# A double layernorm, a two-way Mamba and six transformer layers on one core: Mamba drives of five states by ScalarE and transposes, preceding rows by transfers, a mask in eight products, and met waits between the output products of 68 tiles

## The reference

```
u = layernorm(layernorm(x))                      # the second one affine
for direction in (forward, backward):            # 8 Mamba passes: 4 batches x 2
    xp, z = split(u @ W_in);  xc = silu(conv4(xp) + b)          # 256 channels each
    dt = softplus(...);  B, C = ...              # from xc @ W_x; 16 states
    h[n, t] = h[n, t-1] * exp(dt * A[n]) + (dt * xc) * B[n, t]  # n = 0..15
    y = sum_n h[n, t] * C[n, t] + xc * D;  out_d = (y * silu(z)) @ W_out
x = x + layernorm(x) + 0.5 * (out_f + out_b);  r = layernorm(x)
for layer in range(6):                           # 16 heads of 64
    s = r with the second 64 features taken from the token before
    q, k, v = heads of s @ Wqkv;  q, k = l2norm, scale, rotary
    sim = 8 * q k^T, over a window of 32 tokens and the one before it, masked
    r = r + softmax(sim) v @ Wo;   r = r + gated_feed_forward(layernorm(shifted r))
out = x + r
```

## Time and profile before

| | before |
|---|---|
| runs, median (lowest to highest) | 3920.66 us (3914.4 to 3925.08), 3 runs |
| span of the profiled execution | 3921.5 us |
| busy share: PE, PEld, DVE, ACT, POOL | 95%, 64%, 85%, 74%, 83% |
| first and last scan of the Mamba part | 80.7 us, 1007.9 us |
| first and last score of the transformer part | 1072.7 us, 3864.9 us |

### The profile page before, as it was taken

How to read it: one execution, slowest core, us unless ns; L and a number is a source line. 1 busy time by engine, 2 the same in 40 slices (tenths; PEclk the granted TensorE clock), 3 DMA queues, 4 the chain that set the end, 5 groups by cost and what they waited for, 6 DMA issues and landing times.

```text
span 3921.5 us, 110568 instructions
## 1 busy us (share of the span) xinstructions
PE 3707.5 (95%) x43392; PEld 2518.5 (64%) x43392; DVE 3319.6 (85%) x3407; ACT 2915.4 (74%) x6890; POOL 3241.5 (83%) x2370
## 2 busy tenths in 40 slices
PE   7889989988789999999999999999999999999997
PEld 2333333333377777777777777777767777777775
DVE  4999999999688888888888887888878888788885
ACT  7555445553388887888888887888878888888885
POOL 3888888888698888888888888888888888888883
PEclk8999998998899999999999999999999999999999
DMA  1221222212100000000000000000000000000001
GB/s 68 73 76 70 76 71 75 76 71 83 50 16 2 16 3 2 17 2 16 3 6 13 2 16 2 6 13 3 16 2 6 13 2 16 2 6 2 2 3 44
DMA packets 31567, 102.12 MB, mean 26 GB/s; under 512 B 4676, under 2 KB 6600, under 8 KB 30928
## 3 DMA queue, kind: packets, MB, share of 16 engines
q1 hardware_dynamic: 31056, 95.05, 7.0%
HBM read 90.32 MB, written 4.72 MB: 24 GB/s over the span
## 4 chain that ended last, share of the span: by engine, by line
PE 68%; issue 2%; ACT 2%; DVE 0%; POOL 0%; POOLq 0%; ACTq 0%; DVEq 0%
PE ps L1116 17%; PE ps L1043 13%; PE ps L1105 9%; PE ps L1054 8%; PE ps L1093 7%; PE ps L1141 5%; PE ps L1154 3%; PE ps L1078 2%; PE ps L1065 1%; PE ps L1123 1%; PE ps L1129 1%; ACT prob L1246 0%; PE ps L1023 0%; ACT mixed L1255 0%; ACT w_qk L1175 0%
## 5 line engine op out<-in xcount | busy, mean ns | idle before, releaser
L1521 POOL TENSOR_TENSOR resid<-resid,sq 128x1024 f32<-128x1024 f32 x384 | 910.8, 2377 | 3.4 <-DVE sq L1376 2.9
L626 POOL TENSOR_TENSOR read<-state,c_row 128x1024 f32<-128x1024 f32 x256 | 719.8, 2831 | 153.9 <-DVE state L588 84.9
L1543 POOL TENSOR_TENSOR resid<-resid,rnorm 128x1024 f32<-128x1024 f32 x384 | 725.0, 1904 | 18.1 <-POOL rnorm L1535 0.4
L1116 PE MATMUL ps<-mixed,w_vo 128*128 128x128 f32 x6144 | 720.7, 276 | 3.0 <-ACT mixed L1255 2.8
L1116 PEld LDWEIGHTS ps<-mixed,w_vo 128*128 128x128 f32 x6144 | 711.5, 193 | 12.9 <-issue 4.6
L1043 PE MATMUL ps<-w_qk,xs_parts 128*128 128x512 f32 x2304 | 634.6, 411 | 35.4 <-issue 18.1
L1246 ACT ACTIVATE prob<-ps,stat 128x64 f32<-128x64 f32 x3072 | 653.5, 385 | 0.7 <-DVE stat L1396 0.5
L1376 DVE TENSOR_TENSOR sq<-ps,rope_l 128x1024 f32<-128x1024 f32 x384 | 462.4, 1204 | 101.5 <-ACT sq L1208 101.2
L393 PE MATMUL mamba_ps<-read,ident 128*128 128x512 f32 x1024 | 509.6, 638 | 15.4 <-POOL read L626 15.4
L1389 DVE TENSOR_TENSOR resid<-ps,rope_l 128x1024 f32<-128x1024 f32 x384 | 464.3, 1209 | 66.9 <-ACT sq L1208 59.7
L1043 PEld LDWEIGHTS ps<-w_qk,xs_parts 128*128 128x128 f32 x2304 | 412.4, 191 | 148.6 <-issue 73.8
(11 more groups left out here) (138 smaller groups left out, 5676.8 us busy)
## 6 DMA issues: line engine op xcount, KB each, us to landing
c_row<-c_rows SPq DMA_DIRECT2D x128, 512.0 KB, 3.6
w_stage<-w_qk_hbm SPq DMA_DIRECT2D x12, 512.0 KB, 4.7
vo_stage<-w_v_hbm SPq DMA_DIRECT2D x6, 512.0 KB, 3.7
vo_stage<-w_o_hbm SPq DMA_DIRECT2D x6, 512.0 KB, 4.6
xn<-x_hbm SPq DMA_DIRECT2D x4, 512.0 KB, 6.6
kept<-resid SPq DMA_DIRECT2D x8, 256.0 KB, 4.4
resid<-kept SPq DMA_DIRECT2D x8, 256.0 KB, 4.0
out_hbm<-resid SPq DMA_DIRECT2D x8, 256.0 KB, 2.0
```

The lines of the kernel that those rows point to most:

```text
L626: pool.tensor_tensor(read[:, h, g % 2, :], state[:, h, g % 2, :], c_row[:, g % C_AHEAD, :], ALU.mult).then_inc(done[f"rd{h}"], 1)
L1116: last = pe.matmul(bank[:, 0:P], w_vo[:, l % 2, head_at(place_h), :], mixed[:, odd, place_h, :], start=place_h == 0, stop=place_h == HEADS ...
L1521: pool.tensor_tensor(qk[:, tile % 2, cols], qk[:, tile % 2, cols], sq[:, 1 + part, :], ALU.add).then_inc(done[f"rotated{part}"], 1)
L1543: pool.tensor_tensor(heads, heads, norms, ALU.mult).then_inc(done[f"normed{part}"], 1)
```

## The change

Four things are done, and some small ones.

1. In the Mamba part the drives of states 2, 5, 8, 11 and 14 are no longer made by DVE. Once per sequence PE transposes `dtx` (16 transposes of 128x128, `tt0` to `tt3`) and the rows of B (8 rows deep, `tb`), and ACT copies these (`at0` to `at3`, `ab`). For such a state ACT multiplies the transposed `dtx` by B, which is now a column, in eight 128x256 activations (`td`) into one buffer `drive_t`; PE transposes the product back, eight transposes per half, into a pair of PSUM banks (`p0`, `p1`), and DVE's scan reads that. Those states need no spread row of B. All five order lists and the `FRONT_*` lists are written anew; all layernorm chunks now stand ahead of the first sequence.
2. `row_turn` makes one transpose instead of two. The preceding rows are filled by two transfers per tile from SP (`shift_rows`, 384 in all) into `rows_back`. `copy_rows` copies 128x128, and waits for the transfers of the tile before; `mix` waits for its own tile's.
3. The mask of a tile is eight products with 32 output rows each, in the tiles of 64x32 that the score products have, instead of two with 128.
4. In 68 of the 192 tiles waits for `copy_mixed0`, already met when `output` begins, stand between the 16 output products: 24 to 60 per tile in the built program (53 tiles have 56 or more), 3732 in all, spread over the 15 gaps (60 are four per gap). PE's sequencer reads 97,523 instructions.

Besides, some semaphores are merged and the scratch for dynamic transfers is smaller.

```
-DRIVE_IN_PSUM = (4, 9, 10, 11, 14, 15,)
+DRIVE_IN_PSUM = (4, 10, 15)
+DRIVE_TURNED = (2, 5, 8, 11, 14)
...
+                def turn_drive(h):
+                    def stage(g):
+                        after(pe, ("td", g))
+                        free(f"p{h}", g)
+                        to = drive_of(h, g).rearrange("p c n -> p (c n)")
+                        for j in range(SEQ // P):
+                            last = pe.transpose(to[:, j * P:(j + 1) * P], drive_t[:, j, h * P:(h + 1) * P], ident[:, :])
+                        last.then_inc(done[f"p{h}"], 1)
...
+                def drive_turned(g):
...
+                    after(act, *[(f"at{q}", s) for q in range(TURNS_BY_STATE)], ("ab", s), ("p0", before), ("p1", before))
+                    for j in range(SEQ // P):
+                        last = act.activation(drive_t[:, j, :], dtx_t[:, j, :], ACT.Identity, scale=b_t[:, s % 2, j, n:n + 1])
+                    last.then_inc(done["td"], 1)
...
-                        after(dve, (f"dec{h}", g), (f"dr{h}", g), (f"rd{h}", g - 2))
+                        after(dve, (f"dec{h}", g), (f"p{h}" if g % D_STATE in DRIVE_TURNED else f"dr{h}", g), (f"rd{h}", g - 2))
...
+            def shift_rows(tile):
+                l, t, odd = place(tile)
+                after(sp, ("copy_rows", tile))
+                if tile >= 2:
+                    after(sp, ("mix", tile - 2))
+                before = (tile - 1 if t % SEQ_TILES else tile) % 2
+                sp.dma_start(rows_back[WINDOW:P, odd], rows[0:P - WINDOW, odd]).then_inc(rows_shifted[odd], 16)
+                sp.dma_start(rows_back[0:WINDOW, odd], rows[P - WINDOW:P, before]).then_inc(rows_shifted[odd], 16)
...
-                for back in (WINDOW, 0):
-                    to = bank[:, 0:P] if back else bank[:, P:2 * P]
-                    last = pe.transpose(to, xa[:, first - back:first - back + P], ident[:, :])
-                last.then_inc(done["row_turn"], 1)
+                pe.transpose(bank[:, 0:P], shifted(xa, t * P, P), ident[:, :]).then_inc(done["row_turn"], 1)
...
-                    pe.matmul(ps[:, S + h, :], sight_rows[rows_h, int(t % SEQ_TILES == 0), :], sight_hidden[rows_h, :],
-                              start=True, stop=False, skip_group_check=True)
+                    for w in range(WINDOWS):
+                        queries = slice(w * WINDOW, (w + 1) * WINDOW)
+                        pe.matmul(ps[queries, S + h, :], sight_rows[rows_h, int(t % SEQ_TILES == 0), queries], sight_hidden[rows_h, :],
+                                  start=True, stop=False, skip_group_check=True)
...
+                    spaced = (FETCH_PADS.get(tile, 0) + HEADS - 2 - place_h) // (HEADS - 1) if place_h < HEADS - 1 else 0
+                    for _ in range(2 * spaced):
+                        after(pe, ("copy_mixed0", tile))
```

More of the change, by code:

```diff
@@ L167, in mamba @@
                 (MAMBA_PE, FRONT_PE), (MAMBA_ACT, FRONT_ACT), (MAMBA_DVE, FRONT_DVE), (MAMBA_POOL, FRONT_POOL), (MAMBA_SP, []))]
-        in_sbuf = [g for g in range(2 * BATCH * D_STATE) if g % D_STATE not in DRIVE_IN_PSUM]
+        in_sbuf = [g for g in range(2 * BATCH * D_STATE) if g % D_STATE not in DRIVE_IN_PSUM + DRIVE_TURNED]
         DRIVES, BEFORE = {g: i for i, g in enumerate(in_sbuf)}, dict(zip(in_sbuf[2:], in_sbuf))
@@ L224, in drive_of @@
         def drive_of(h, g):
+            if g % D_STATE in DRIVE_TURNED:
+                first = SLOTS[f"p{h}", g][0]
+                return ps[:, first:first + 2, :]
             if h:
@@ L373, in b_rows, with turn_dtx, stage, turn_b @@
                     last.then_inc(done["b"], 1)
+                def turn_dtx(q):
+                    def stage(s):
+                        after(pe, ("tx0", s), ("tx1", s))
+                        to = free(f"tt{q}", s)
+                        for j in range(2):
+                            for h in range(HALVES):
+                                first = (2 * q + j) * P
+                                last = pe.transpose(to[:, (2 * j + h) * P:(2 * j + h + 1) * P], dtx[:, s % 2, h, first:first + P],
+                                                    ident[:, :])
+                        last.then_inc(done[f"tt{q}"], 1)
+                    return stage
+                def turn_b(s):
+                    after(pe, ("abc0", s), ("abc1", s))
+                    to = free("tb", s)
+                    for j in range(SEQ // P):
+                        last = pe.transpose(to[:, j * D_STATE:(j + 1) * D_STATE], x_dbl[0:D_STATE, j * P:(j + 1) * P],
+                                            ident[0:D_STATE, 0:D_STATE])
+                    last.then_inc(done["tb"], 1)
+                def turn_drive(h):
[6 more added lines that the diff above has]
+                        last.then_inc(done[f"p{h}"], 1)
+                    return stage
                 def add_skip(h):
@@ L408, in _ @@
                           "b": b_rows, **halved("sk", add_skip), **halved("y", add_read),
-                          **banked("o", output)}
+                          **banked("o", output), **{f"tt{q}": turn_dtx(q) for q in range(TURNS_BY_STATE)}, "tb": turn_b,
+                          **halved("p", turn_drive)}
                 for name, k in PE_SEQ:
@@ L484, in stage @@
                     def stage(s):
-                        after(act, (f"bc{c}", s), ("split", s - 1), ("cst", s - 1), *[(f"dt{h}{k}", s - 1) for h in range(HALVES) for k in range(2)])
+                        after(act, (f"bc{c}", s), ("split", s - 1), ("cst", s - 1), ("tb", s - 1), *[(f"dt{h}{k}", s - 1) for h in range(HALVES) for k in range(2)])
                         act.copy(x_dbl[:, cols(c)], bank(f"bc{c}", s)[0:BC_ROWS + DT_RANK]).then_inc(done[f"abc{c}"], 1)
@@ L495, in stage @@
                         def stage(s):
-                            after(act, (f"dt{h}{c}", s), (f"tx{h}", s - 2), (f"dr{h}", D_STATE * (s - 1) - 1))
+                            after(act, (f"dt{h}{c}", s), (f"tx{h}", s - 2), (f"dr{h}", D_STATE * (s - 2) + LAST_SPREAD),
+                                  *[(f"tt{q}", s - 2) for q in range(TURNS_BY_STATE)])
                             act.activation(tile[:, s % 2, h, cols(c)], bank(f"dt{h}{c}", s), func,
@@ L514, in softplus_log, with take_turned, stage, take_b @@
                     return stage
+                def take_turned(q):
+                    def stage(s):
+                        after(act, (f"tt{q}", s), ("td", D_STATE * (s - 1) + LAST_TURNED))
+                        act.copy(dtx_t[:, 2 * q:2 * q + 2, :], bank(f"tt{q}", s).rearrange("p (j n) -> p j n", j=2)
+                                 ).then_inc(done[f"at{q}"], 1)
+                    return stage
+                def take_b(s):
+                    after(act, ("tb", s), ("td", D_STATE * (s - 2) + LAST_TURNED))
+                    act.copy(b_t[:, s % 2, :, :], bank("tb", s)[:, 0:SEQ // P * D_STATE].rearrange("p (j n) -> p j n", n=D_STATE)
+                             ).then_inc(done["ab"], 1)
+                def drive_turned(g):
+                    s, n = divmod(g, D_STATE)
+                    k = DRIVE_TURNED.index(n)
+                    before = D_STATE * s + DRIVE_TURNED[k - 1] if k else D_STATE * (s - 1) + LAST_TURNED
+                    after(act, *[(f"at{q}", s) for q in range(TURNS_BY_STATE)], ("ab", s), ("p0", before), ("p1", before))
+                    for j in range(SEQ // P):
+                        last = act.activation(drive_t[:, j, :], dtx_t[:, j, :], ACT.Identity, scale=b_t[:, s % 2, j, n:n + 1])
+                    last.then_inc(done["td"], 1)
                 def decays(h):
@@ L624, in stage @@
                         if g < 2:
-                            after(pool, ("naf", TOKENS // BANK - 1))
+                            after(pool, *[("naf", 2 * (2 * h + g) + c) for c in range(HALF_BANKS)])
                         pool.tensor_tensor(read[:, h, g % 2, :], state[:, h, g % 2, :], c_row[:, g % C_AHEAD, :],
@@ L856, in transformer @@
     newton = sb("newton", [P, 2 * HEADS])
-    rows = sb("rows", [P, 2, 2, P])
+    rows = sb("rows", [P, 2, P])
+    rows_back = sb("rows_back", [P, 2, P])
     qk = resid.rearrange("p (o n) -> p o n", o=2)
@@ L907, in ff_added, with shifted_back @@
         eng.wait_ge(x_ready, chunk + 1)
+    def shifted_back(eng, tile):
+        eng.wait_ge(rows_shifted[tile % 2], 32 * (tile // 2 + 1))
     def indexed(name, f, n):
@@ L967, in _ @@
                 l, t, odd = place(tile)
-                after(sp, ("copy_rows", tile))
+                shift_rows(tile)
                 if t == LOAD_W1_AT:
@@ L1100, in mix @@
                 after(pe, ("turn_probs", tile), ("copy_rows", tile))
+                shifted_back(pe, tile)
                 banks = [turn_free("mix", tile, w) for w in range(WINDOWS)]
-                for own in range(2):
+                for own, of in enumerate((rows_back, rows)):
                     for w in range(WINDOWS):
                         rows_w = slice(w * WINDOW, (w + 1) * WINDOW)
```

(6 more changed lines are left out.)

114 lines of the change are left out of this document (60 added, 54 removed), and 106 rows, old and new, of tables (FETCH_PADS, FRONT_ACT, FRONT_DVE, MAMBA_ACT).

## The result

The changed kernel takes 4046.7 us (4038.4 to 4050.5) against 3922.1 us of the kernel before: 1.031 of it, interval 1.030 to 1.032. Slower was forecast, but by 1.0%, not 3.1%. The profiled execution has a span of 4036.6 us, 115.1 above that of before. It is the fastest of four; the medians are 124.6 us apart, and where the other 10 us lie is not known.

A forecast was written before the change was run, and what follows sets the result against it. PE was taken to bound the transformer part, and DVE, with PE 3% behind, the Mamba part. On 3921.5 us, -50 + 4 - 17 - 18 - 5 + 125 = +39 gave 3960 us; own range 3932 to 3990, wider range 3860 to 4015.

The forecast's parts named there:

- The met waits (+125): Output stages: waits at 0.11 us each outlast the products between them, less the sequencer's lead; +125 us, bounds 0 to 175.
- Rival (a): Output stages: the waits cost nothing, as passes are queued while a wait runs; 3835.5 us, chance 0.16.
- the lead in the first tile of a chunk: Output stages: time from the sequencer's last wait ahead of the stage to its start; 0.2 us in tile 108.
- The fetch term (-5): A -5 us entry in the forecast's sum, for instruction fetching; its reasoning is not in the prediction as given.
- The Mamba part (-50, and +4 ahead of it): Mamba part: DVE relieved, PE becomes the bound at 110.4 us per sequence, -50 us; layernorm chunks before the first scan +4.
- the prediction's own sign: Mamba part: first to last scan shorter by about 50 us, with PE's busy share above DVE's.
- the range that I gave (106.6 to 114.3): Mamba part: PE's need per sequence after the change, 106.6 to 114.3 us.
- Row turn (-17): Row turn: one 0.11 us transpose fewer per tile, partly given back at the output stage; -17 us, bounds 0 to -21.
- mask (-18): Mask stage: the mask in the scores' own tiles removes 0.1 us at the tiling change; -18 us, bounds 0 to -18.
- Transfers: Row turn: the transfers of preceding rows cost nothing, `copy_rows` feeding `mix` 16.5 us later; no PE wait for `rows_shifted`.
- The waits' upper bound of 175: Output stages: 53 x 3.3 us = 175 us, if the sequencer's lead doesn't help.

The follow-up runs named there:

- the ladder: Changed kernel with one to six met waits per gap in layers 0 to 5: first-tile output stages late by 0.01, 0.34, 1.93, 3.54, 5.29, 7.20 us.
- the two shift runs: Kernel before with 128 or 256 more instructions, met waits in the Mamba part's `b_rows`: 3965.2 us (1.011) and 3915.5 us (0.998).
- the run that took 50 us of it away: Changed kernel without met waits, six of eight first-half SBUF scans reading the second half's drive in PSUM: 3910.7 us, first to last scan 889.7 against 900.7.

## Why the prediction was wrong

**The met waits (+125), which carried the forecast, were right in mechanism and too small.** They cost 161.7 us in the output stages. The 37 us above the forecast are the largest single miss; without them 4046.7 would be 4010, inside the range. Rival (a), in which they are free, is refuted by the ladder. Each stage was late by 0.4 to 0.6 us more than forecast (3.6, 1.7, 3.0, 2.3 against 3.1, 1.1, 2.6, 1.9). In that step I took the product time for the 15 products between the waits and let the sixteenth start at once; in the trace 0.4 us pass from the last wait to the next stage, 0.22 of which the product is. The pace over a whole stage is 0.117, not 0.11, and the lead in the first tile of a chunk 0.07 instead of 0.2. That lead was read in the kernel before, where a second row transpose ran ahead of the output stage; with the waits alone it is 0.17, so I had priced the row turn and the waits as if they didn't touch. Over the 53 tiles with 56 or more it makes 154 us against 119. (Two slips of the sum matter little: 60 x 0.11 is 6.6 and not 6.65, and the rows give tile 111 a lead of 1.3 us and not 1.4; neither moves the term by more than 3 us.)

**The fetch term (-5) failed in its premise.** I took the stops of the kernel before as those that the changed kernel would have, and bounded the term by them at 7 us. But every instruction added or removed moves the boundaries of the 256-instruction blocks in all stages behind it, and the kernel before lies near the best of the positions that were run: with 128 instructions more its score stages take 41 us longer, with 256 the same. I worked out the position of each score stage's first instruction in its block from the instruction order, for ten kernels, and compared it with the time of the stage and the 14 passes behind it. In third tiles the mean hold-up is at most 0.03 us for positions 32 to 159, and 1.3 to 1.7 from 176 to 239; the other places lose at most some 0.5 us, from 192 on. In the kernel before 3 of 48 third tiles lie at 160 or above or under 32; in the changed kernel without waits 23 do. (That such a stage waits for the fetching of the next block is inferred from the period of 256; the profile calls it "issue".) So the change without its waits would have lost 31 us in score stages, and the waits win that back: the term should have been two, +31 from the change and -31 from the waits, where I had -5.

The Trainium skill, in Runtime: NRT & Kernel Launch, under Instruction fetch mechanics, gives blocks of 256 instructions, which the 381 blocks of the changed kernel's 97,523 instructions bear out (the profile page's row: packets, MB, share). It also calls the crossing of a boundary mostly hidden. For the output stages, where a pass takes 0.11 us, that is so here: the two shift runs differ by 1.8 us in them. For score stages, 256 instructions in 1.4 us, they differ by 42.

```profile
q8 instruction: 381, 6.24, 0.7%
```

**The Mamba part (-50, and +4 ahead of it)** gave -27 and +9.3. The step that failed is that PE becomes the bound: from the first to the last scan DVE is still the busier, 869.5 of 902 us against 842.1, where the prediction's own sign was PE's share above DVE's. That 112.5 us per sequence lies in the range that I gave (106.6 to 114.3) is luck, as that range was PE's need. What I left out is that DVE loses too: the 64 scans with a drive in SBUF are a microsecond longer (3301 ns in the mean against 2268), 66 us of the 90 taken off DVE, and its busy time fell by 17. The earlier trace rows held the sign of it, reads of 2816 ns; I read it as POOL's load and didn't ask who would wait when POOL is no longer the one that comes second. How much of the missing 23 us this explains stays open: the run that took 50 us of it away got 11 back. What the higher granted clock gave was not tried either.

**Row turn (-17) and mask (-18)** came out at -20.1 and -17.3 in their own stages. Some 6 to 8 us of it return in the head turns that follow a row turn behind the scores; that cause was not tried. Transfers cost nothing that shows: the larger ones land 1.9 us after their issue, and no PE wait is put down to them.

```profile
rows_back<-rows SPq DMA_DIRECT2D x192, 48.0 KB, 1.9
```

**The sum as measured:** -19.5 ahead of the first score, -20.1, -17.3, +161.7, 0 in the score stages, +10.3 in the rest: +115.1 on the span. Three errors had the same sign, 37 us in the waits, 26 ahead of the first score and 15 in what I had at -5 for fetching and at nothing for the rest, so the range (to 4015), which let one term miss at a time, was too narrow. The waits' upper bound of 175 I had thought possible only if the lead were worthless; it wasn't, and they still cost 162.

## What to carry to other kernels

A met wait between short products is not free: set its pace, start to start, against the time of the product that is to cover it, and count the sequencer's lead; here two waits per 0.22 us product all but hide, and each further one costs 0.1 us. In a stream with stretches of instructions that are much shorter than the rest, a change of the number of instructions anywhere moves the time of code that it doesn't touch: compare such kernels at the same position modulo 256, or a gain (here 8 us of the new Mamba part) looks like a loss of 22. When work is taken off an engine that wins a contended resource, look at who starts first afterwards.

## What was not expected of the hardware

Adding 256 met waits to the kernel before did not slow it (0.998), and adding 128 cost 1.1%. The hold-up can fall into the `mix` behind a score stage instead (404.5 us against 379.4 with 3737 spread waits), or once into both (3.54 us for a `mix` of 2.00); nothing in the profile names a cause but "issue". And a scan with both inputs in SBUF takes between 2264 and 4470 ns: over 2.30 us only where a POOL read was running when it began, in 48 of 64.
